# One drain on GpSimd between the scatters of the seventh and the eighth expert, in an attention and mixture-of-experts kernel

## The reference

```
weights = golden_weights(x, Wr, temperature)          # (b, t, 8), zero for experts a token does not use
gate = einsum('btd,edf->betf', x, Wg)
up   = einsum('btd,edf->betf', x, Wu)
h    = silu(gate) * up
e_out = einsum('betf,efd->betd', h, Wd)
out   = einsum('bte,betd->btd', weights, e_out)
x = x + out
```

## Time and profile before

| what | value |
|---|---|
| median of 3 runs | 738.79 us |
| lowest and highest run | 738.13 and 738.86 us |
| span of the profiled execution | 734.8 us |
| median less span | 4.0 us |
| POOL busy | 400.4 us of the span |
| PE busy | 622.5 us of the span |

### The profile page before, as it was taken

One profiled execution on the slowest core, in us unless ns is written; L12 is line 12 of the kernel. 1 busy time (PEld: TensorE's weight loads), 2 busy tenths in 40 slices (PEclk: granted clock), 3 DMA queues, 4 the chain that ended last, 5 costly groups with the idle time before them and its releaser, 6 DMA issues.

```text
span 734.8 us, 15767 instructions
## 1 busy us (share of the span) xinstructions
PE 622.5 (85%) x5300; PEld 326.1 (44%) x5300; DVE 567.8 (77%) x928; ACT 460.4 (63%) x552; POOL 400.4 (54%) x446
## 2 busy tenths in 40 slices
PE   6999999667867777777767677799999999999992
PEld 3444443233534334443434346455555555555551
DVE  4997778999999999999999997683736637356330
ACT  6344358788889989898989896233534435344321
POOL 5264356636577878787877771224335443354403
PEclk9999999999999999999999998899999999999997
DMA  7777767999989999999999995259797887967804
GB/s 251 197 150 168 167 142 117 185 188 188 172 170 198 189 193 194 188 192 189 195 190 186 192 174 170 60 201 237 170 245 119 242 235 176 246 156 211 137 5 57
DMA packets 318516, 129.42 MB, mean 176 GB/s; under 512 B 293508, under 2 KB 293508, under 8 KB 318472
## 3 DMA queue, kind: packets, MB, share of 16 engines
q1 hardware_dynamic: 311296, 112.64, 71.4%
q0 software_dynamic: 7168, 16.26, 10.7%
q10 hardware_dynamic: 8, 0.01, 0.0%
HBM read 44.33 MB, written 12.06 MB: 77 GB/s over the span
## 4 chain that ended last, share of the span: by engine, by line
PE 49%; issue 13%; DVE 8%; DMA 8%; ACT 7%; SPq 6%; POOL 6%; POOLq 1%; ACTq 0%; DVEq 0%
PE psum L1601 44%; DMA work<-work 7%; ACT work L1020 5%; DVE spare L1325 2%; POOL work L666 2%; DVE spare L1334 2%; SPq L477 2%; SPq L475 2%; SPq L444 1%; PE psum L1831 1%; PE psum L1764 1%; PE psum L1910 1%; PE psum L1825 1%; PE psum L1606 1%; DMA token_region<-values_region 1%
## 5 line engine op out<-in xcount | busy, mean ns | idle before, releaser
L1020 ACT ACTIVATE work<-spare,exp_bias 128x2048 uint8<-128x2048 f32 (+1 forms) x128 | 255.1, 1994 | 30.1 <-POOL exp_bias L672 20.4
L1334 DVE TENSOR_SCALAR_CACHE_REDUCE spare<-psum,q_step_now 128x1024 f32<-128x1024 f32 x128 | 162.2, 1271 | 1.8 <-PE psum L1764 1.7
L666 POOL CAST work<-work 128x2048 int16<-128x2048 uint8 x70 | 132.4, 1892 | 38.1 <-DMA work<-work 31.5
L1325 DVE TENSOR_SCALAR_CACHE_REDUCE spare<-psum,q_step_now 128x2048 f32<-128x2048 f32 x64 | 150.1, 2345 | 0.7 <-PE psum L1764 0.5
L1764 PE MATMUL psum<-keys_region,work 128*128 128x512 f16 x256 | 73.7, 389 | 43.9 <-DVE spare L1334 26.6
L798 POOL DMA_INDIRECT work<-x_rows,slot_tok x32 | 51.3, 1602 | 103.8 <-DVE slot_w L1533 74.5
L1764 PE MATMUL psum<-keys_region,bias_hl 128*128 128x512 f16 x256 | 70.8, 382 | 28.5 <-DVE spare L1334 23.0
L810 POOL DMA_INDIRECT out_dram<-keys_region,slot_tok x32 | 51.7, 1616 | 72.7 <-ACT keys_region L1097 65.6
L1724 PEld LDWEIGHTS psum<-values_region,work 128*128 128x128 f16 x2048 | 66.0, 96 | 37.6 <-POOL work L666 20.9
L1724 PE MATMUL psum<-values_region,work 128*128 128x32 f16 x2048 | 70.8, 177 | 12.0 <-DMA work<-work 4.4
L1601 PE MATMUL psum<-work,spare 128*128 128x480 f16 (+1 forms) x396 | 79.2, 360 | 0.9 <-DVE work L1506 0.9
(11 more groups left out here) (226 smaller groups left out, 1014.8 us busy)
## 6 DMA issues: line engine op xcount, KB each, us to landing
spare<-in_L_ffn_Wd_dram SPq DMA_DIRECT2D x8, 1024.0 KB, 15.4
spare<-in_L_ffn_Wg_dram SPq DMA_DIRECT2D x7, 1024.0 KB, 5.8
spare<-in_L_ffn_Wu_dram SPq DMA_DIRECT2D x7, 1024.0 KB, 11.3
work<-in_ctx_dram SPq DMA_DIRECT2D x3, 1024.0 KB, 5.8
work<-work SPq DMA_TRANSPOSE x174, 3.6
token_region<-in_L_xattn_Wkv_dram SPq DMA_DIRECT2D x2, 1024.0 KB, 6.2
resid<-in_x_dram SPq DMA_DIRECT2D x2, 1024.0 KB, 8.8
out_dram<-work SPq DMA_DIRECT2D x8, 256.0 KB, 2.6
```

The lines of the kernel that those rows point to most:

```text
L666: nc.gpsimd.tensor_copy(p_T_int[h % 4], pair_bytes[h % 4]).then_inc(unpacked, 1)
L1020: nc.scalar.activation(p_out, scores, ACT.Exp, bias=exp_bias[:, h % 4:h % 4 + 1], scale=-1.0, accum_out=p_sum[:, h:h + 1]).then_inc(exp_do ...
L1325: nc.vector.tensor_scalar(staged[h % 4], psum[:, at:at + 4, :].rearrange("p b k -> p (b k)"), q_step_now[:, h:h + 1], None, ALU.mult, ALU.min,
L1334: nc.vector.tensor_scalar(staged[h % 4][:, 1024 * c:1024 * c + 1024], psum[:, at:at + 2, :].rearrange("p b k -> p (b k)"), q_step_now[:, h ...
```

## The change

```diff
@@ -822,6 +822,7 @@
                 last = E // 2 - 1 + i0
                 gather(last, 1)
                 scatter(last, 0)
+                nc.gpsimd.drain()
                 scatter(last, 1)
 
             def rows_added(k):
```

## The result

| | before | changed |
|---|---|---|
| median | 738.65 us of 8 runs (738.0 to 740.9) | 735.08 us of 8 runs (732.79 to 738.63) |
| span of the profiled execution | 734.8 us | 731.5 us |
| ratio to before | | 0.9946, 95% interval 0.9924 to 0.9968 |

The change makes the kernel faster, by 0.5 to 0.7%. The median falls by 3.6 us where 4.85 were forecast. A second set of 11 runs gave 734.62 us against 738.73, 4.1 us less, and a ratio of 0.9928 (0.9904 to 0.9953), which is 5.3 us of 738.7. One execution of the kernel before, beside the last three experiments, took 1219.12 us for an unknown reason, and no ratio takes it in.

A forecast was written before the change was run, and what follows sets the result against it. GpSimd's closing DRAIN of 5303 ns was taken to bound the kernel's end. Shortening it saves 4.85 us, the added DRAIN is hidden and costs nothing: 738.79 - 4.85 = 733.9 us, range 732.9 to 735.4, forecast's chance 76 in 100.

The forecast's parts named there:

- The bound of the end: Kernel's end, after the last landing at 729.0 us: everything waits for GpSimd's closing DRAIN of 5303 ns.
- The price: GpSimd's DRAIN: it settles each software DMA issued since the last DRAIN, at 80 to 83 ns each.
- 0.18 us for an idle drain: GpSimd's DRAIN at the program's start: 179 ns with no software DMAs behind it, partly wait for memsets.
- The cover: POOL's 22.36 us idle before the eighth expert's scatter: hides the added 5.0 us DRAIN with 12.7 us to spare.
- The rule: Skill page on opening and closing DRAINs: constant about 12 ns on all engines, so nothing saved and 738.8 us.
- One term of the sum: Whole run: the median of the runs lies 4.0 us over the profiled span of 734.8 us.
- The signs: Changed profile: added DRAIN about 5.0 us, closing 0.33 to 0.50 us, eighth scatter at 717.8, last landing 729.0, span 730.0.
- A fixed price: Closing DRAIN: costs 5.3 us whether 4 or 64 software DMAs are behind it; 738.8 us; chance 10 in 100.
- a price paid once: First DRAIN after software DMAs pays whatever their number; closing one 0.18 us or less; 733.7 us; chance 5 in 100.
- Half and half: Closing DRAIN: 2.6 us fixed, the rest by DMA, so 2.8 us remains; 736.3 us; chance 5 in 100.
- a drain that does nothing: Closing part: DRAINs are always cheap, the 5.3 us is the closing part's own wait; 738.8 us; chance 2 in 100.
- outlast its cover: Added DRAIN before the eighth scatter: slowed by busy engines, at factor 6 it gives 746.2 us; chance 2 in 100.

The follow-up runs named there:

- the last three experiments: Against the kernel before: a drain between branch and last landing waits (736.47 us), the change plus that drain (734.33 us), a drain inside the eighth expert's scatter (740.93 us).
- The increment in its place: Kernel before with a semaphore increment nobody waits for where the change puts its drain: 739.73 us, ratio 1.0009.
- the loop: Kernel before with a drain behind every expert's scatter but the last: 734.47 us, ratio 0.9928.
- the repeated set: The changed kernel measured again with no further edit, 11 runs: 734.62 us against 738.73 us for the kernel before.
- the second drain: Kernel before with two drains in a row between the seventh and eighth experts' scatters: 736.71 us in one run.

## Why the prediction was right

**The bound of the end.** The last 5.3 us were GpSimd's closing DRAIN and nothing else. The increment in its place left it at 5303 ns, and every kernel with an earlier drain shortened it.

**The price.** This was only argued from two rows. The closing DRAINs now make a table:

| software DMAs since the last DRAIN | closing DRAIN, ns |
|---|---|
| 0 | 52 to 60 |
| 3 | 307 |
| 4 | 382 to 392 |
| 8 | 719 |
| 60 | 4962 |
| 64 | 5303 |

From 4 to 64 it is (5303 - 392) / 60 = 82 ns a DMA, beside 50 to 60 ns for a drain with none. The prediction's 80 to 83 ns hold, for DMAs of this size (120 or 128 rows); a price by bytes would fit nearly as well, as said above. Its 0.18 us for an idle drain was too high, as it supposed, since that row had memsets in it. The forecast gain on this instruction was 4.80 to 4.97 us; it is 5303 - 392 = 4.91 us.

**The cover.** It was costed at nothing, and is: 22.37 us idle, ended by ACT. The added DRAIN ended 6.6 us after the last issue's end. The prediction had allowed 8.9 us (704.3 less 695.43), by landing first and settling then. That was too cautious: the drains end 6.9 and 6.4 us after the last issue's end with 64 DMAs behind them, 6.5 to 6.6 with 60, 6.2 with 61, 6.1 with 56, and 4.4 with 8. At 82 ns a DMA, those with 56 to 64 begin to settle 1.2 to 1.7 us after the last issue's end; the ones with 8 to 12 are bound by the flight of their last scatter (4.4 us at the end of the kernel, 7.5 to 8.0 us in the loop). What the 1.2 to 1.7 us are, and why they vary, is open. The prediction also put ACT's busy time in the cover at about a third; it is less than a quarter, which changes nothing.

**The rule.** The Trainium skill, "VectorE: DVE Perf Modes", section "The DRAIN you can't avoid", has about 12 ns for the DRAINs of a program's ends on all five engines. In the closing part it was 12 to 13 ns on SyncE, 69 to 82 ns on DVE, PE and ACT, and on GpSimd 52 to 60 ns at best and 5303 ns with 64 software DMAs to settle. The measurement decides. The page calls them the runtime's own, and that the block's closing part is one of them is the prediction's reading.

**The size.** By the medians the gain was 3.6 us in the first set and 4.1 us in the second; by the ratios' intervals it is 2.4 to 5.6 us in the first and 3.5 to 7.1 us in the second. The 4.9 us of the trace lie within both. The runs scatter by more than the gain's own uncertainty (731.12 to 740.02 in the repeated set), so the rows are the sharper measure. One term of the sum was wrong. The median was put 4.0 us over the span, as if the profiled execution were a typical one. In every run on record that has a span the time is 1.7 to 1.9 us over it (733.33 and 731.5, 740.02 and 738.2). So the profiled execution of before was probably one of about 736.6 us, 2 us faster than its median. The predicted time was not hurt, since it subtracts from the median. The signs that it gave as times of the profile were not met: the eighth scatter was to start at 717.8, the last landing to come at 729.0 and the span to be 730.0, and they were 719.45, 730.6 and 731.5. All three are the slower stretch near 475 us, which the prediction did not reckon with. That 735.08 us lies in the range, by 0.3 us, is in part luck. The range took the scatter of runs as 0.7 us, from three of them, and eight of the changed kernel scatter by 5.8 us.

**The rivals.** A fixed price falls with the closing 392 ns, and a price paid once with the 719 ns for eight DMAs. Half and half falls with the second drain's 47 ns, a drain that does nothing with 8.5 us and 392 ns. The changed kernel's drain did not outlast its cover, and other engines' work did not stretch the settling (4972 ns for 60 DMAs beside a busy PE, 4962 ns on an empty machine). But covers of under 10 us in the other places were outlasted, by 1.1 us ahead of the seventh scatter and by 0.1 us in the loop. What was long there was the wait for gathers or scatters still in flight.

## What to carry to other kernels

Look at what stands behind the last landing, and ask for the closing part by its line, because the engine's busy time leaves it out. If GpSimd has issued many DMAs of its own, a drain in its last long idle stretch takes 82 ns for each of them off the end (for DMAs of the size here). The stretch must outlast the flight of the last of them and most of the settling: the drains here ended 4.1 to 8.0 us after the last issue. One is enough; it must have nothing urgent queued behind it on GpSimd, not even a branch.

## What the runs showed of the hardware that was not expected

- A GpSimd DRAIN costs 47 to 60 ns with nothing behind it and 82 ns for each software DMA of about 0.25 MB since the last one, gather or scatter (404 ns, and 382 to 392 ns, for four), on an idle machine and beside a busy PE.
- It settles DMAs while later ones are in flight (6.4 to 6.9 us from the last issue's end with 64 behind it, where landing and settling in turn would need 9.2 us). With 8 to 12 behind it, it ends 0.4 to 0.5 us after the last landing.
- A drain holds POOLq: a load and a branch behind it cost 1.3 us that had been hidden.
- The 28 executions of the kernel before in one set differ by up to 10 us, and part of such differences is where the granted clock falls: 12 equal matmuls took 1.39 us at clock 1.00 and 2.60 us in a stretch at 0.66.
